# A small fill behind every scatter of the expert stage, on one core of a Trainium2 chip

## What is computed

```
x = x + tanh(g_ffn) * ffn(layernorm(x), ...)

gate_logits = einsum('ble,en->bln', x, gate_kernel)
top_k_weights, top_k_indices = top_k(gate_logits, 2)
softmax_probs = softmax(top_k_weights)
layer_mult = silu(einsum('ble,neh->blnh', x, w0_kernel)) * einsum('ble,neh->blnh', x, w1_kernel)
intermediate = einsum('blnh,nhe->blne', layer_mult, wo_kernel)
output = einsum('blne,bln->ble', intermediate, weights)
```

## Time and profile before

| | |
|---|---|
| median of 3 runs | 662.53 us |
| the profiled execution | 666.6 us, of which its instructions span 664.6 us |
| TensorE busy | 572.5 us (86%) |
| ScalarE busy | 413.9 us (62%) |
| VectorE busy | 403.2 us (61%) |
| GpSimd busy | 379.5 us (57%) |
| scatters L1095 | 142, mean 1005 ns |
| scatters L1046 | 128, mean 999 ns |

### The profile page before, as it was taken

How to read it: one execution, slowest core, us unless ns; L and a number is a source line. 1 busy time by engine, 2 the same in 40 slices (tenths; PEclk the granted TensorE clock), 3 DMA queues, 4 the chain that set the end, 5 groups by cost and what they waited for, 6 DMA issues and landing times.

```text
span 664.6 us, 20166 instructions
## 1 busy us (share of the span) xinstructions
PE 572.5 (86%) x5930; PEld 465.1 (70%) x5931; DVE 403.2 (61%) x1356; ACT 413.9 (62%) x1083; POOL 379.5 (57%) x520
## 2 busy tenths in 40 slices
PE   5999999999999998989999974988889888898870
PEld 3776777777677776767667763877777777787760
DVE  4687887888787876876888751622223323332773
ACT  2677787777777876867887762554444544454540
POOL 3135666665665665565566476655555555565661
PEclk9999999999999998998999997899999999999995
DMA  3551121212121211211211132322222222225986
GB/s 75 172 150 50 51 69 53 71 48 63 56 64 48 71 48 44 67 53 46 65 54 56 45 97 92 102 73 76 72 80 76 76 73 79 79 77 158 287 258 213
DMA packets 70245, 57.95 MB, mean 87 GB/s; under 512 B 8966, under 2 KB 66062, under 8 KB 70192
## 3 DMA queue, kind: packets, MB, share of 16 engines
q1 hardware_dynamic: 52240, 35.92, 19.2%
q0 software_dynamic: 8640, 16.93, 7.6%
q10 hardware_dynamic: 9312, 4.46, 2.3%
HBM read 29.84 MB, written 24.15 MB: 81 GB/s over the span
## 4 chain that ended last, share of the span: by engine, by line
PE 65%; another core or an unknown queue 9%; DVE 7%; issue 7%; ACT 6%; DMA 2%; ACTq 1%; DVEq 1%; POOL 1%; SPq 0%; POOLq 0%
PE psH L531 13%; PE psH L451 9%; PE psH L437 8%; PE psO L503 6%; PE psH L443 6%; PE psK L481 4%; PE psG L545 3%; PE psO L545 3%; DVE mx L843 3%; PE psO L476 2%; PE psO L477 2%; PE psO L465 2%; PE psX L459 2%; PE psK L462 1%
## 5 line engine op out<-in xcount | busy, mean ns | idle before, releaser
L1095 POOL DMA_INDIRECT results<-ys,zin x142 | 142.7, 1005 | 101.3 <-ACT ys L685 58.4
L1046 POOL DMA_INDIRECT lists<-zp,dest x128 | 127.9, 999 | 63.0 <-DVE dest L858 32.6
L531 PE MATMUL psH<-zT,wcur 128*128 128x256 f32 x568 | 138.4, 387 | 16.2 <-ACT wcur L672 13.2
L531 PEld LDWEIGHTS psH<-zT,wcur 128*128 128x128 f32 x568 | 103.3, 192 | 32.9 <-ACT wcur L672 15.3
L604 ACT ACTIVATE ex<-psH,rs 128x512 f32<-128x512 f32 x128 | 81.9, 685 | 67.8 <-PE psH L443 55.6
L963 DVE TENSOR_TENSOR hm<-psH,hs 128x512 f32<-128x512 f32 x71 | 49.0, 691 | 99.8 <-PE psH L531 35.9
L843 DVE TENSOR_REDUCE mx<-psH 128x8 fp32r<-128x512 f32 x128 | 82.6, 685 | 21.7 <-PE psH L437 18.4
L503 PEld LDWEIGHTS psO<-v,pT 128*64 128x64 f32 x2048 | 67.1, 137 | 32.2 <-issue 17.3
L1077 POOL TENSOR_TENSOR kvr<-ropA,ropB 128x256 f32<-128x256 f32 x64 | 46.6, 728 | 67.7 <-DVE ropB L920 63.4
L503 PE MATMUL psO<-v,pT 128*64 128x64 f32 x2048 | 77.6, 226 | 5.6 <-issue 5.4
L608 ACT COPY pT<-psH 128x512 f32<-128x512 f32 x128 | 71.7, 591 | 12.1 <-PE psH L451 11.9
(11 more groups left out here) (153 smaller groups left out, 979.6 us busy)
## 6 DMA issues: line engine op xcount, KB each, us to landing
zin<-lists SPq DMA_DIRECT2D x71, 130.0 KB
yy<-results SPq DMA_DIRECT2D x16, 512.0 KB
xres<-x1r SPq DMA_DIRECT2D x32, 128.0 KB, 2.2
out_dram<-xres ACTq DMA_DIRECT2D x16, 256.0 KB
xring<-in_x_dram SPq DMA_DIRECT2D x31, 128.0 KB
cring<-in_ctx_dram SPq DMA_DIRECT2D x31, 128.0 KB
results<-ys,zin POOLq DMA_INDIRECT x142
lists<-pad SPq DMA_DIRECT2D x16, 130.0 KB, 4.1
```

What stands on the lines that cost most here:

```text
L531: last = pe.matmul(bank[t.buf(2)][:, k * ET:(k + 1) * ET], wcur[:, t.buf(2), a, k * P:(k + 1) * P], zT[:, t.buf(2), :], start=True, stop=True)
L1046: nc.gpsimd.indirect_dma_start(lists, bass.IndirectOffsetOnAxis(ap=dest[:, t.buf(4), j:j + 1], axis=0), zp[:, t.buf(4), j, :], None).then_ ...
L1095: nc.gpsimd.indirect_dma_start(results, bass.IndirectOffsetOnAxis(ap=zin[:, t.buf(8), h, D:D + 1].bitcast(U32), axis=0), ys[:, t.buf(8), h ...
```

## The change

GpSimd gets a tile of its own, `apart` (128 partitions x 128 float32), and a semaphore, `apart_done`. Behind each of the two scatters of a tile it waits until its previous fill is done (for the first scatter of a tile that is the second fill of the tile before, for the second the first fill of the same tile), then an empty instruction, and then it fills `apart` with zeros. Nobody reads the tile, and no other engine waits for the semaphore.

```diff
@@ -251,6 +251,7 @@
         first_row = sb("first_row", [P, NET])
         table = sb("table", [P, 2, NET], U32)
         warm = sb("warm", [P, 1])
+        apart, apart_done = sb("apart", [P, D]), sem("apart_done")
         zin = sb("zin", [P, 8, 2, ROW])
         zT = sb("zT", [P, 2, ET])
         wcur = sb("wcur", [P, 2, 2, HID])
@@ -1095,6 +1096,12 @@
                             nc.gpsimd.indirect_dma_start(
                                 results, bass.IndirectOffsetOnAxis(ap=zin[:, t.buf(8), h, D:D + 1].bitcast(U32), axis=0),
                                 ys[:, t.buf(8), h, :], None, bounds_check=NOWHERE - 1, oob_is_err=False).then_inc(y_out[t.buf(8)], 16)
+                            if h:
+                                wait_for(pool, apart_done, t, per=2, part=0)
+                            else:
+                                wait_for(pool, apart_done, t, back=1, per=2)
+                            carry(pool)
+                            nc.gpsimd.memset(apart[:, :], 0.0).then_inc(apart_done, 1)
 
                 EXPERTS.run(pool, experts_step)
```

## The result

The median of nine runs after the change is 657.95 us (655.58 to 661.78), beside nine of the kernel before with 662.53 (661.08 to 667.2). The ratio is 0.9923, with a 95% interval of 0.9896 to 0.995: faster by 4.6 us going by the medians (5.1 going by the ratio) where 19 were forecast. It lies in the forecast range of 627 to 670, but above the forecast's own range of 628 to 657. The profiled execution took 659.45 us, its span is 657.6.

A forecast was written before the change was run, and what follows sets the result against it. Bound: TensorE's news held behind scatters drained at 1.43 us each. Profiled 666.6 us, -20 (gain), +1 (end) make 647.6; the median lies 4.1 lower, so 643.5 us. Range 627 to 670, the forecast's own 628 to 657.

The forecast's parts named there:

- The bound: Expert stage: news of finished matmuls waits behind a backlog of scatters, costing 0.62 us of 3.46 us a tile.
- The spacing: Between GpSimd's scatter starts in the expert stage: the fill adds 0.09 us, from 1.29 to 1.38 us.
- The wait: GpSimd's wait for its previous fill, behind each scatter: costs nothing, or up to 0.74 us a scatter if cover is gone.
- The third rival: The wait empties GpSimd's queue, 4.0 us a tile in the expert stage, GpSimd the bound: 701 us, chance 0.06.
- The gain: Expert stage, 65 tiles: half of the 40 us lost to held news goes, -20 us, bounds 0 and -40.
- the first rival: Scatters still drain at 1.43 us each, so releases don't move and only the end's +1 us stays: 663.5, chance 0.20.
- the idle time until "remote": Sign of the gain: ScalarE's and VectorE's idle time before ys and zT falls to about half.
- The chain's pieces without an owner: Sign of the gain: pieces of 2.17 to 3.67 us in the expert stage get shorter than 2 us.
- The fourth rival: The fill breaks the backlog altogether if spacing reaches 1.43 us; expert stage at 2.84 us a tile: 623.5, chance 0.10.
- The second rival: Release follows the last scatter's start by 1.9 us, so runs grow longer, +10 us with the end: 672.5, chance 0.22.
- The end: The last eight scatters lie on the path: seven gaps of 0.09 us, taken as +1 us, at most 1.4.
- The port: Fills may collide with VectorE's 32 two-input additions at the end, 0 to +6 us; left out of the sum.

The follow-up runs named there:

- fill512: The changed kernel with fills of 512 columns in place of 128: 663.37 us, ratio 1.0001 to the kernel before.
- alloc_only: The changed kernel with its tile and semaphore kept but the waits and fills removed: 662.47 us, ratio 0.9996 to the kernel before.
- fill256: The changed kernel with fills of 256 columns in place of 128: 657.68 us, ratio 0.9924 to the kernel before.
- after_copy: The changed kernel without any edit, profiled on a chip where the kernel before takes about 589 us: 591.81 us, ratio 1.0044.

## Why the prediction was right in its direction and wrong in its size

**The bound: right.** The forecast took the loss to be news of TensorE held behind scatters, 0.62 us a tile, from 3.46 and 2.84. On the chips where nothing is held the same kernel has 2.83 us a tile and is 74 us faster; the expert stage's part, first scatter to last, is 242.7 us against 571.33 - 375.97 = 195.4. That compares two chips. On the same chip, fill512 shows that the held news goes with the spacing of the scatters, but not what the stage would take without it, because there GpSimd is the bound.

**The spacing: right.** 1.38 forecast, 1.37 measured, with a fill of 0.24 us where I had 0.20.

**The wait: right.** It costs no idle time: 0.16 or 0.17 us before a scatter. The third rival (701 us) fell.

**The gain: mis-sized, at the step "so I take half of the loss".** That was -20 us; what the medians show is -4.6, and the two profiles have -2.2 in the expert stage. The step took the stretch in the earlier trace rows for the effect of a spacing. Three things in it failed.

- The drain of 1.43 us a scatter, which I had worked out myself, held: 5.73 us for a run of four before, 5.75 after, 8.5 to 8.6 for a run of six at 1.29 (runs of two are slower, 1.5 a scatter). By it nothing moves at a spacing of 1.37. That was the first rival, with 0.20, and for the full releases it is what happened. I argued against it from a single stretch of four scatters, in which the pairs happened to come 2.84 us apart and which had the same 5.81 us as the rest. The stretch showed what a lighter load looks like, not what a spacing brings.
- What the change did bring was a term that the prediction didn't have, the half releases: 8 from 450 to 590 us where there were 3, each 0.7 us earlier. Those three stood in the trace before; I had taken all news to be let through at once. 5 x 0.7 = 3.5 us is an estimate of what they can give in that stretch; the windows view gives 11 records more, 0.61 of a tile or 2.1 us, but alloc_only has 12 fewer than before without being slower. So the sizes don't contradict each other, and that the half releases make the gain was only argued. Why there are more of them at 1.37 is open.
- I had named the idle time until "remote" as the thing that would halve. It rose from 31.2 to 45.1 us before ys and from 37.8 to 45.0 before zT. The chain's pieces without an owner, which I said would be shorter than 2 us, are still mostly about 3. From the chain of after, in order of time (13 pieces from 443 to 632 us):

```profile
443.20 3.11 another core or an unknown queue
...
486.75 3.75 another core or an unknown queue
```

**The fourth rival, all of the loss goes at 1.43: wrong too.** fill256, at 1.48, has 3.37 us a tile, not 2.84, and its news is still held. Of the spacings tried where news is held, only at 1.69 was it free, and there GpSimd sets the pace.

**The second rival, the release follows the last scatter by 1.9 us:** fell. In full releases of a run of four it is 1.56 to 1.77 in after, against 1.81 to 1.93 in before; what grew in the one shrank in the other, as the drain has it.

**The end: small, as forecast, at this level.** The last run of after has six scatters and not eight. From its first start to its last (635.25 to 642.38) it takes 7.1 us, where the last six of before take 6.9, and from there to the end of the span it is 0.2 us more: 0.4 in all where I had +1. On the faster chips the packed end is 29 gaps long rather than 7, and there it is the whole of the change: +2.6 us. On the chip where the changed kernel was timed at that level "slower", by 0.4%, is thus the true answer, by a mechanism whose price per gap was in the prediction and whose length wasn't.

**The port:** the fill took 0.24 us with VectorE at work and 0.20 at the kernel's start, so at most 0.04 us of it can be the port. The rule that spoke against the change had fills meeting VectorE's additions at the end. Eleven fills of after do, and they take 0.24 to 0.25 us like the others. What is lengthened is the scatter that starts under an addition (1.33 us at 616.66 in before, 1.45 at 547.08 in after_copy), which the kernel before has as well. The Trainium skill (Perfetto Trace Analysis, GPSIMD Engine Instruction) says to time GpSimd's operations by the spacing of their starts rather than by their reported spans. The traces agree: the span of most scatters is 0.98 us in every kernel while the spacing goes from 1.29 to 1.69, and 0.98 and 0.24 don't make 1.37 by themselves.

## What to carry to other kernels

A chain with unowned pieces, and two engines that wait for different results and start together behind a run of indirect DMAs, suggest that semaphore news is held; count the releases from the first of the run. A law that fits (here 1.43 us a scatter) tells which part of the wait a smaller spacing can't move. It doesn't tell that the law holds beyond the spacings it was read from: at 1.48 it failed. Don't read the effect of a change from one stretch that happens to look like it: ask first what number in that stretch would have to differ, and whether it did. And run the kernel before under a profile on a second chip early: this change gains 0.8% against something that not every chip does, and costs 0.4% where it isn't there.

## What the runs showed of the hardware that I had not expected

- The same one-core program took 662.9 us on one chip and 588.8 to 589.5 on three others (medians), 12% apart, with a granted clock of 1.00 in the expert stage at both levels. On the slower one finished matmuls became known late behind scatters. In the run of twelve of the earlier trace rows the matmuls of L545 into psO end at 401.23 us and ScalarE's ys starts at 413.75, 12.5 us later, of which it sat idle for 8.67. The run doesn't hold all news until its end: another operation of ScalarE is released in the middle of it. On the other chips ScalarE started 0.04 us behind its matmuls, with scatters in rows of over twenty. Why the chips, or what ran on them then, differ so is open. The rows in the kernel before:

```profile
400.18 1.05 PE L545 MATMUL psO<-wo,hm 128*128 x8
...
404.48 0.60 ACT L678 ACTIVATE hs<-psH 128x512 f32<-128x512 f32 x1 [3.52 <-remote]
```

- The held news of a run comes out at about 1.43 us per scatter from the run's first (1.5 in runs of two), or 0.6 to 1.2 us behind a scatter's start. At a spacing of 1.69 us nothing was held, on the same chip and with GpSimd busy for 90% of the time.
- A scatter that starts while VectorE runs an addition with both inputs in SBUF ends about 0.86 us behind the end of that addition (0.85 to 0.87) and takes up to 1.45 us instead of 0.98. A fill of 128 columns in the same place keeps its 0.24 to 0.25.
- A scatter of 128 rows of 512 bytes has a spacing of 1.29 us; a fill behind it makes it 1.29, 1.37, 1.48, 1.58 or 1.69 for 1, 128, 256, 384 or 512 columns: the first 128 are nearly hidden, then each further 128 cost 0.11.
- On a chip that holds nothing, 80 fills of 0.24 us cost nothing outside of the stage's packed end, and in that end 29 gaps with a fill cost 2.9 us, 0.08 each and the rest in lengthened scatters.
